# Graph gathers: GpSimd waits for the preceding chunk's rows between a chunk's first gather and its other three

## The reference

```
x = x + graph attention 0(layernorm(x), src, dst, edge_attr)
x = x + sliced attention FFN(layernorm(x))
x = x + graph attention 1(layernorm(x), src, dst)
x = x + mixture of 8 experts, top 2 of them (layernorm(x))
```

```
h = x @ W.T                                   (layer 1: x itself)
alpha = s_src[src] + s_dst[dst] (+ edge term relu(edge_attr @ edge_W.T + edge_b) . h[dst] in layer 0)
alpha = where(alpha >= 0, alpha, 0.2 * alpha)
ex = exp(alpha - segment_max(alpha, dst)[dst])
out[n] = sum over edges with dst = n of  h[src] * ex / segment_sum(ex, dst)
```

## Time and profile before

| | us |
|---|---|
| median of 2 timed runs | 4188.9 (4188.48 to 4189.31) |
| span of the profiled execution, first to last instruction | 5182.1 |

### The profile page before, as it was taken

How to read it: one execution, slowest core, us unless ns; L and a number is a source line. 1 busy time by engine, 2 the same in 40 slices (tenths; PEclk the granted TensorE clock), 3 DMA queues, 4 the chain that set the end, 5 groups by cost and what they waited for, 6 DMA issues and landing times. The chain is left out here.

```text
span 5182.1 us, 77256 instructions
## 1 busy us (share of the span) xinstructions
PE 3347.4 (65%) x13712; PEld 2377.0 (46%) x13713; DVE 2375.1 (46%) x5239; ACT 1277.0 (25%) x5289; POOL 2286.8 (44%) x2343
## 2 busy tenths in 40 slices
PE   4500676767777777598935545554555537999998
PEld 3300343444444444365823333333333335889887
DVE  4500566656666666776434444444444436111111
ACT  2200333333333333242300000000000034333333
POOL 5160555555555555200355555555555540333333
PEclk9855888888888888798967777777777757999999
DMA  8441333333333333200133333333333342666665
GB/s 200 127 127 32 81 81 76 82 76 81 84 83 81 81 79 83 49 0 1 47 78 86 82 84 85 85 86 84 84 85 85 85 124 96 172 171 171 172 171 136
DMA packets 298776, 489.07 MB, mean 94 GB/s; under 512 B 151906, under 2 KB 199984, under 8 KB 298216
## 3 DMA queue, kind: packets, MB, share of 16 engines
q0 software_dynamic: 127312, 325.41, 25.7%
q1 hardware_dynamic: 158637, 158.21, 10.4%
q10 hardware_dynamic: 12770, 4.81, 0.4%
HBM read 430.09 MB, written 58.63 MB: 94 GB/s over the span
## 5 line engine op out<-in xcount | busy, mean ns | idle before, releaser
L826 POOL DMA_INDIRECT g_rows<-rows,g_recs x1856 | 1759.0, 948 | 1562.6 <-DVE g_msg L980 832.2
L864 PE MATMUL g_pA<-g_msg,k_ident 128*128 128x264 f32 x3712 | 1102.1, 448 | 150.8 <-DVE g_msg L980 91.1
L864 PEld LDWEIGHTS g_pA<-g_msg,k_ident 128*128 128x128 f32 x3712 | 795.0, 225 | 501.3 <-issue 360.7
L855 PE MATMUL g_pE<-g_ew,g_recT 128*128 128x512 f32 x936 | 597.0, 772 | 419.3 <-ACT g_recT L895 373.7
L866 PE MATMUL g_pA<-g_accs,k_ident 128*128 128x264 f32 x928 | 353.6, 467 | 663.4 <-DVE g_accs L987 517.0
L980 DVE TENSOR_TENSOR g_msg<-g_rows,g_pp 128x1024 f32 (+1 forms) x464 | 564.9, 1218 | 417.4 <-ACT g_pp L920 332.3
L915 ACT ACTIVATE g_msg<-g_dd (+1 forms) x464 | 113.5, 245 | 1827.8 <-DVE g_dd L1023 1228.3
L866 PEld LDWEIGHTS g_pA<-g_accs,k_ident 128*128 128x128 f32 x928 | 185.6, 220 | 766.2 <-DVE g_accs L987 570.8
L855 PEld LDWEIGHTS g_pE<-g_ew,g_recT 128*128 128x128 f32 x936 | 202.7, 233 | 648.4 <-issue 584.6
L1969 PE MATMUL e_pY<-e_w,e_hT 128*128 x1632 | 375.1, 383 | 22.6 <-issue 21.9
L1958 PEld LDWEIGHTS e_pH<-e_xT,e_w 128*128 128x128 f32 x3264 | 382.3, 193 | 5.2
(11 more groups left out here) (410 smaller groups left out, 3575.4 us busy)
## 6 DMA issues: line engine op xcount, KB each, us to landing
e_w<-in_L_ffn_W SPq DMA_DIRECT2D x110, 1024.0 KB
g_rows<-rows,g_recs POOLq DMA_INDIRECT x1856
g_recs<-slots SPq DMA_DIRECT2D x468, 8.0 KB
tok<-e_xall SPq DMA_DIRECT2D x7, 910.0 KB
rows<-p_row SPq DMA_DIRECT2D x50, 119.0 KB
own<-p_row SPq DMA_DIRECT2D x50, 119.0 KB
p_x<-in_x SPq DMA_DIRECT2D x1, 5600.0 KB
own<-p_x SPq DMA_DIRECT2D x1, 5600.0 KB
```

Of the source, the lines that this page charges most:

```text
L826: pool.indirect_dma_start(out=rows[:, r, j, :], out_offset=None, in_=rows_d, in_offset=bass.IndirectOffsetOnAxis(ap=recs[:, r, 4 * j:4 * j ...
L855: last = t_.matmul(pE[:, b, c:c + 512], recT[:, b, :], ew[:].rearrange("p c d -> p (c d)")[:, c:c + 512], start=True, stop=True)
L864: t_.matmul(pA[:, b, 0:MW], K["ident"][:], msg[:, b, j, :], start=(j == 0), stop=False)
```

## The change

Before the second gather (j == 1) of every chunk but the very first, POOL now waits until all rows of the preceding chunk have landed, and increments the semaphore pace, as it does after its other waits. pr and pu are the buffer and the group of the preceding chunk. The other gathers, their order, the buffers and all other engines stay as they are.

```diff
@@ -823,6 +823,10 @@
                             pool.wait_ge(msg_ok, 4 * (u - 1) + (r + 1))
                             pool.sem_inc(pace, 1)
                         for j in range(C):
+                            if j == 1 and not (first and r == 0):
+                                pr, pu = (r - 1) % R, (u if r > 0 else u - 1)
+                                pool.wait_ge(rows_in[pr], 16 * C * (pu + 1))
+                                pool.sem_inc(pace, 1)
                             pool.indirect_dma_start(out=rows[:, r, j, :], out_offset=None, in_=rows_d,
                                                     in_offset=bass.IndirectOffsetOnAxis(ap=recs[:, r, 4 * j:4 * j + 1].bitcast(I32), axis=0)
                                                     ).then_inc(rows_in[r], 16)
```

## The result

The changed kernel takes 4833.7 us (2 runs, 4832.25 to 4835.17) against 4188.9 us: 645 us more, ratio 1.154 with a 95% interval of 1.151 to 1.157. The forecast was 4675 us, range 4430 to 4780. Direction and mechanism came out, the size did not: the forecast is 159 us too low, and the time lies above its range.

The account below looks back on a forecast made before the run. POOL's gathers were taken to bound both graph layers; landing 2.82 plus restart 0.78 less 2.50 us gave 1.10 us per chunk, 255 us in layer 1 and 231 in layer 0: 4189 + 486 = 4675 us, range 4430 to 4780.

Parts of the forecast that it names:

- The pace before: Both graph layers: POOL's gathers set the pace, 4 x 1.25 = 5.00 us per chunk, about 5.05 in the mean.
- rival A: Buffers before a chunk's first gather: slack hides the new wait, not slower, 4189 us; chance 0.08.
- The queue instructions cost nothing: POOL's queue: the added wait and increment themselves cost nothing, as queue instructions run ahead while a gather executes.
- A plain boundary: Between chunks: second gather starts 3.60 instead of 2.50 us after the preceding fourth, 1.10 us more per chunk.
- Term 1, the landing: At the new wait: preceding chunk's fourth gather start to all rows landed, 2.82 us; ends 0.95 and 3.1 us.
- rival D: Landings at the new wait: one chunk in four lands 1.8 us later, 4883 us; chance 0.05.
- Term 2, the restart: POOL after the new wait: 0.78 us to start a gather with an empty queue; ends 0.30 and 0.81 us.
- the forecast's discount in layer 0: Layer 0: POOL and consumers hold each other up, 5.10 us per chunk before, 6.10 after, so 1.00 us more.
- B: Chunk boundaries: those where POOL waits for g_msg hide the wait, only 249 pay, 4463 us; chance 0.15.
- C: Landings at the new wait: 2.32 us in timed runs, half a microsecond sooner than recorded, 4467 us; chance 0.08.

Follow-up runs that it names:

- e14: Kernel before, unchanged, profiled in an undisturbed job: 4195.4 us beside 4191.2 us, span 4193.7 us.
- e1: Kernel before, unchanged, profiled once more in a disturbed job: 5146 us, beside timed runs of the same kernel of 5124 us.
- e15: Changed kernel with its wait for the rows of the chunk two before, undisturbed: 4191.3 us beside 4191.2 us, ratio 0.9997.
- e12: Changed kernel with empty edge slots spread over 16 padding rows, undisturbed: 4717.1 us beside 4187.8 us, ratio 1.1264.
- e7: Changed kernel with its wait before the first gather of a chunk, disturbed: 5548.4 us beside 5196.7 us.
- e10: Changed kernel with its wait in every second chunk only and empty slots spread over 16 padding rows, undisturbed: 4432.9 us, ratio 1.0568.
- e11: Changed kernel with its wait before the third gather and empty slots spread over 16 padding rows, undisturbed: 4190.9 us, ratio 0.9992.
- e6: Kernel before with empty edge slots spread over 16 padding rows, no added wait, disturbed: 5182.5 us beside 5183.7 us, ratio 0.9992.
- e3: Changed kernel with empty edge slots spread over 16 padding rows, disturbed: 4864.1 us beside 5124.0 us.
- e5: Changed kernel as it is, run in a disturbed job: 4996.8 us beside 5183.7 us, ratio 0.9635.
- e8: Kernel before with POOL filling a 128x1024 scratch tile between each chunk's first and second gather, disturbed: 4976.4 us beside 5196.7 us, ratio 0.9566.

## Why the prediction was wrong in size

**The pace before.** Right. The forecast reconciled a 5182 us span with a 4189 us time by dropping the stalls, took POOL's 4 x 1.25 = 5.00 us for the pace and put the mean at 5.05; e14 has 5.03. The sentence that "the recording cost 993 us" was wrong, though: e1 shows that it is the job, not the recording. In a disturbed job the slack of rival A is real, and more than that, the changed kernel is faster there (0.9635), which none of the rivals had.

**The queue instructions cost nothing.** Right, within what can be measured: 0.9997 (0.9988 to 1.0007) in e15.

**A plain boundary.** Right: 3.60 us forecast, 3.61 in the rows above. Over e12, without the 16 long restarts and the last boundary of each layer, the mean from the fourth gather to the next second one is 3.59 us in layer 0 and 3.56 in layer 1, so a plain boundary costs 1.09 and 1.06 us against 1.10. The order of the gathers' starts and the idle time of 1.4 us came as said. The dose bears the rule out: a wait at the first gather costs 1.17 us more than at the second (e7), at every second chunk about half (e10), at the third nothing (e11).

**Term 1, the landing.** This is the step that failed: "I take 2.82 us", with 3.1 us as the upper end "where undisturbed". It took a typical landing for the mean. The time of a wait is the mean over all landings, and 80 of the 462 aren't typical: the mean is 3.07 us. Of the 645 us, 117 are late landings (changed kernel against e12). The row that could have told was in view, 1221.19 to 1225.8, 4.6 us: it is one of the gathers whose 128 slots are all empty. The forecast used it for rival D alone, at a chance of 0.05 and a price of 4883 - 4675 = 208 us for one chunk in four, and laid it to chip or recording. It was neither: it is the data. A landing that nobody waited for directly cost nothing before (e6: 0.9992, in a disturbed job), so no wait of POOL in the profile of before pointed to it. But SP waits for every chunk's landing: in that trace L796 lets go over 3.3 us after the fourth gather's start at 96 of 464 chunks, which single rows don't show and a count over all of them does.

**Term 2, the restart.** 0.78 us is right for 446 of the 462 waits. The other 16 restarts took 3.3 us, 2.5 more each, 40 us in all, with which the mean is 0.86 and 0.84 us. The forecast had no such case, and its cause is open. e10 bears the size out: it meets none of the 16, and (529 - 40)/2 = 245 us is near the 239 us that it cost.

**The sum of the miss.** 159 us = 117 for late landings + 42: 4717.1 against 4675. The 42 are +40 for the long restarts, +23 for the forecast's discount in layer 0 (1.00 instead of 1.10 us, unfounded by e14: 5.04 us per chunk before, not 5.10) and +3 for the last boundary of each layer, less 10 because plain boundaries are a little shorter than 3.60 us, and less 14 for small pauses above the 1.25 us beat that POOL has in e14 anyway and that the waits take in. These parts are estimates, added up from the starts of all gathers of e12 and e14.

**The rivals.** B (4463) and C (4467) fell: no boundary was hidden, and no typical landing came sooner. C's 2.32 us was also what the fit of the Trainium skill gave, "DMA: Bandwidth & Descriptors", section "Anatomy of one DMA — SWDGE (gpsimd) path": about 2.0 us plus bytes over 436,000 per us, for 139 KB an estimate of 2.3 us. In both kinds of job SP is let go 2.8 us after the gather's start, so the measurement decides. D had the right kind of event, late single landings, but the wrong origin and a price of 208 us where 117 were measured. A (4189 us) fell with the timed runs; its slack is there in a disturbed job only.

No version here beats the kernel before where it takes 4189 us. In disturbed jobs e3 (4864 us) was the best of all that were run.

## What to carry to other kernels

A wait put into an issuing engine's queue costs landing plus restart minus the work already issued behind the awaited transfer; one gather more of distance made 529 us (e12 beside 4187.8) into nothing (e11). Take the mean of the landing, and of the restart, from all transfers and look for classes among them: padding that points many descriptors at one row made some gathers land 4.8 instead of 2.8 us after their start, at no cost until something waited. And where span and timed runs of a kernel differ by a quarter, get a profile of the right kind before pricing stalls: the sign of this change depended on it.

## What was not expected of the hardware

- A gather of which all, or nearly all, of the 128 descriptors read one and the same row of 1088 bytes in HBM lands late, and the later the more of them follow one another. By the DMA records of the changed kernel the last packet of the first such gather comes 3.4 us after its start in the mean, that of the third in a row 4.2 us (median of all gathers 2.45). The fourth gather above, the third in its row, lets POOL go at 4.8 us instead of 2.8 us. Spread over sixteen rows, such gathers land like any other (e12: 3.52 us from the fourth gather to the next second one, not 5.57). What in the memory makes it so was not looked into.
- The same kernel, in different jobs, takes 4188 to 4194 us or 5124 to 5197 us, on the same chips. In the second kind queue instructions of SP, ACT and DVE, but none of POOL and PE, take 0.7 us instead of 0.02 by the hundreds, most of them in the two layers, while gathers follow one another. Waiting for landings at each chunk's first or second gather cuts 1415 of them (e1) to 174 (e5) and 175 (e7), a pause of 0.83 us without a wait to 1244 (e8). Why is open.
- With the wait before the second gather of every chunk, POOL restarts at every 26th chunk 3.3 us after the wait has ended and not 0.78 (16 times each in e12 and in the changed kernel, about 40 us). Why is open.
